# Moving the output product behind the probability transposes, and the value product ahead of the next scores, in a two-pass transformer kernel

## The reference

```python
def _layer(x, wqkv, qs, ksc, wo, lg, lb, w1, b1, w2, b2):
    h = shift_token(x)                      # second half of the columns comes from the row above
    q, k, v = split(h @ wqkv, 3)            # 8 heads of 64
    q, k = l2norm(q) * qs, l2norm(k) * ksc
    q, k = rotary_xpos(q, k)
    o = local_attention(q, k, v)            # windows of 128 rows, own window and the one before
    x = x + o @ wo
    h = layernorm(shift_token(x)) * lg + lb
    a, g = split(h @ w1 + b1, 2)
    return x + (a * gelu(g)) @ w2 + b2
```

## Time and profile before

| | before |
|---|---|
| median of 3 runs | 2546.14 us (2543.6 to 2547.74) |
| the profiled execution | 2547.59 us, of which the span of its instructions is 2545.8 us |
| granted TensorE clock, mean | 0.999 |
| busy: TensorE, VectorE, ScalarE, GpSimd | 98%, 77%, 71%, 61% |

### The profile page before, as it was taken

How to read it: one execution, slowest core, us unless ns; L and a number is a source line. 1 busy time by engine, 2 the same in 40 slices (tenths; PEclk the granted TensorE clock), 3 DMA queues, 4 the chain that set the end, 5 groups by cost and what they waited for, 6 DMA issues and landing times. The chain is left out here.

```text
span 2545.8 us, 80138 instructions
## 1 busy us (share of the span) xinstructions
PE 2489.4 (98%) x29664; PEld 2227.2 (87%) x29664; DVE 1969.8 (77%) x6501; ACT 1816.6 (71%) x5192; POOL 1565.2 (61%) x1799
## 2 busy tenths in 40 slices
PE   8999999999999999999999999999999999999999
PEld 7789888888899889998777888999999988999998
DVE  7888788777777887777655887777777788778886
ACT  5778777777777777776454778777777777777775
POOL 5666666666666666665212667666666667666665
PEclk9999999999999999999999999999999999999999
DMA  3121011003000000005101000000003100000000
GB/s 125 35 85 66 26 57 55 27 21 122 15 2 2 2 2 27 3 9 202 36 19 35 2 2 2 2 2 2 2 2 114 43 3 19 19 19 19 19 19 27
DMA packets 75958, 82.21 MB, mean 32 GB/s; under 512 B 37553, under 2 KB 61873, under 8 KB 74417
## 3 DMA queue, kind: packets, MB, share of 16 engines
q1 hardware_dynamic: 74272, 75.61, 9.1%
...
## 5 line engine op out<-in xcount | busy, mean ns | idle before, releaser
L634 POOL TENSOR_TENSOR pr<-pr,rden 128x384 f32<-128x384 f32 (+1 forms) x480 | 409.4, 870 | 316.3 <-DVE rden L1766 314.3
L842 ACT ACTIVATE pr<-pr,nb 128x192 f32<-128x192 f32 (+1 forms) x1024 | 438.0, 430 | 158.9 <-DVE nb L1757 158.9
L1147 PE MATMUL bank<-h2T,w 128*128 128x256 f32 x1408 | 405.3, 288 | 4.0
L1148 PE MATMUL bank<-h2T,w 128*128 128x256 f32 x1408 | 395.1, 281 | 0.0
L1149 PE MATMUL bank<-h2T,w 128*128 128x256 f32 x1408 | 395.1, 281 | 0.0
L1757 DVE CUSTOM_DVE_ANT_0 pr<-bank,maskb,r 128x192 f32<-128x192 f32 (+1 forms) x1024 | 348.0, 396 | 19.6 <-PE bank L1210 7.9
L676 POOL TENSOR_TENSOR uTl<-t,uTh 128x256 fp32r<-128x256 f32 x288 | 219.5, 767 | 190.7 <-ACT uTh L942 157.6
L1147 PE MATMUL bank<-wqkv,hT 128*128 128x512 f32 x768 | 304.4, 396 | 1.9 <-DVE nb L1757 1.9
L1148 PE MATMUL bank<-wqkv,hT 128*128 128x512 f32 x768 | 302.6, 394 | 0.0
L1149 PE MATMUL bank<-wqkv,hT 128*128 128x512 f32 x768 | 299.8, 390 | 0.0
L1147 PEld LDWEIGHTS bank<-h2T,w 128*128 128x128 f32 x1408 | 266.6, 189 | 11.9 <-DVE h2T L1799 10.5
...
## 6 DMA issues: line engine op xcount, KB each, us to landing
...
stt<-stt SPq DMA_DIRECT2D x256, 3.0 KB
...
stt<-stt SPq DMA_DIRECT2D x192, 0.0 KB
```

The lines of the kernel that those rows point to most:

```text
L634: e.tensor_tensor(probs(j, t), probs(j, t), rden[:, 2 * j:2 * j + 2].unsqueeze(2).to_broadcast([P, 2, w]), ALU.mult).then_inc(pn_done, 1 i ...
L842: last = e.activation(probs(j, t)[:, g, :], probs(j, t)[:, g, :], ACT.Exp, bias=nb[:, hd:hd + 1], scale=-1.0, accum_out=den[:, hd:hd + 1])
L1147: e.matmul(out, left[0], right[0], start=first, stop=False)
L1148: e.matmul(out, left[0], right[1], start=False, stop=False)
```

## The change

It reorders the queues of four engines; no instruction that computes is added or removed, and the sums are the same.

- TensorE: WO of the tile before, which stood between S and A1, goes behind PTE (t = 3) or behind A0 (t = 1, 2). In t = 1 and 2, PV goes behind A2 and the rest of W2, so that the next tile's S follows it. In t = 3 q is transposed ahead of k. In t = 0 two units of W2 go between the transposes of k and of q. W1's job 6 makes the products with the high part of h2T first.
- ScalarE: the square of k goes between the second and the third pair of exponentials (in all tiles; it was so in t = 0 only), without its wait for VectorE's rotary terms. O of the tile before stands behind the exponentials in t = 2 and 3, O_first at the end.
- VectorE: O of the tile before is behind k's chain (t = 2, 3), O_add behind the second reciprocal; k's squares are summed ahead of the third rotary step; the addition of WO and the statistics go behind q's chain.
- GpSimd: the guard of k's norm (`guard_k`) is ahead of the last NP; XB goes behind k's chain in t = 0.
- The small orders: entry normalization and the b1 corrections move by a step or two.

TensorE's queue in an ordinary sequence, from the transposes of t = 2 to its end: before. `h2T`, `hT`, `oT` name the input of W1, A1, WO; `t` is k or q, `pr` the probabilities, `ident` marks a transpose.

The diff, cut to its core:

```diff
@@ -604,6 +604,11 @@
...
         def _(e):
+def guard_k(L, b, t):
+    m = idx(L, b, t)
+    e.wait_ge(ssk_done, at(ssk_done, m + 1))
+    e.tensor_scalar(ssg[:, 0, :], ssk[:, :], 1e-24, None, ALU.max).then_inc(guarded, 1)
 def A1_k(L, b, t):
@@ -611,9 +616,6 @@
...
-    e.wait_ge(ssk_done, at(ssk_done, m + 1))
-    e.tensor_scalar(ssg[:, 0, :], ssk[:, :], 1e-24, None, ALU.max).then_inc(guarded, 1)
     e.wait_ge(guarded, at(guarded, 2 * m + 1))
@@ -683,16 +685,20 @@
...
     for j in range(4 if t else 3):
-        if prev and t == 0 and j == 2:
-            XB(*prev, t)
+        if t == 0 and j == 2:
+            guard_k(*ahead)
         NP(L, b, t, j)
+        if ahead and t and j == 2:
+            guard_k(*ahead)
     if ahead:
         A1_k(*ahead)
+    if prev and t == 0:
+        XB(*prev, t)
     if t == 3:
...
         A1_q(*ahead)
-    if L == 0 and b < 2 and t == 1 - b:
+    if L == 0 and b < B - 1 and t == (1 if b < 2 else 0):
         entry_rstd(b + 1)
@@ -801,11 +806,9 @@
...
-def A1_k(L, b, t, turned=False):
+def A1_k(L, b, t):
     m = idx(L, b, t)
     e.wait_ge(k_ps, at(k_ps, m + 1))
-    if turned:
-        e.wait_ge(rotk, at(rotk, m + 1))
     e.wait_ge(ssk_done, at(ssk_done, m))
@@ -951,33 +954,37 @@
...
         S(L, b, t, j)
-        if t == 0 and j == 1:
+        if ahead and j == 1:
             A1_k(*ahead)
-    if ahead and t:
-        A1_k(*ahead, True)
+    if t > 1:
+        O(L, b, t - 1)
     if ahead:
         A1_qv(*ahead)
-    if L == 0 and b == 0 and t == 2:
-        entry_apply(1, 0)
+    if L == 0 and b < 2 and t == 2:
+        entry_apply(b + 1, 0)
     for a in pair:
...
         A0(*ahead2)
-    if t:
+    if t == 3:
         O_first(L, b, t)
-    if t == 3:
         O(L, b, t)
-    if ahead:
+    if ahead and t == 3:
+        A2_q(*ahead)
+        A2_k(*ahead)
+    elif ahead:
         A2_k(*ahead)
         A2_q(*ahead)
-    if t < 3:
+    if t == 0:
         O(L, b, t)
+    elif t < 3:
+        O_first(L, b, t)
     if t == 3:
...
     if L == 0 and b < B - 1:
-        for k in ((), (0, 1), (2, 3), ())[t] if b else ((), (), (1,), (2, 3))[t]:
+        for k in ((), (0, 1), (2, 3), ())[t] if b > 1 else ((), (), (1,), (2, 3))[t]:
             entry_apply(b + 1, k)
@@ -1220,8 +1227,10 @@
...
         e.wait_ge(pt_sb, at(pt_sb, 3 * n - 2 + a))
-    if j == 0:
+    if j == 0 and t < 2:
         e.wait_ge(o_lo, at(o_lo, 2 * n))
+    elif j == 0:
+        e.wait_ge(o_added, at(o_added, sums(L, b, t - 1) + 2))
     if j == 0 and t == 0:
@@ -1326,7 +1337,17 @@
...
         e.wait_ge(u_done, at(u_done, 12 * b + (96 * L + job - 3)))
-    for g in range(2 if mt < MT - 1 else 1):
+    if job == 6:
+        out = bank[job % 4][:, 0:256]
+        for k in range(KT):
+            for s_ in range(HL):
+                e.matmul(out, w1[:, k, s_, mt * P:(mt + 1) * P], shifted(h2T, 0, k, half * 2 * P, 2 * P),
+                         start=(k == 0 and s_ == 0), stop=False)
+        e.wait_ge(h2t_lo, at(h2t_lo, 2 * b + (16 * L + 2)))
+        for k in range(KT):
+            mm = e.matmul(out, w1[:, k, 0, mt * P:(mt + 1) * P], shifted(h2T, 1, k, half * 2 * P, 2 * P),
+                          start=False, stop=(k == KT - 1))
+    for g in range(0 if job == 6 else 2 if mt < MT - 1 else 1):
         for k in range(KT):
@@ -1389,7 +1410,7 @@
...
         ahead2 = (L, b, t + 2) if t < NT - 2 else nxt and (*nxt, t - 2)
-        cuts = ((5, 6, 11, UNITS), (0, 0, 7, UNITS), (0, 0, 7, UNITS), (0, 0, 7, UNITS))[t]
+        cuts = ((5, 6, 11, 13, UNITS), (0, 0, 7, UNITS), (0, 0, 7, UNITS), (0, 0, 7, UNITS))[t]
@@ -1399,8 +1420,6 @@
...
     S(L, b, t, 1, bool(nxt))
-    if t:
-        WO(L, b, t - 1)
     fill(0)
@@ -1415,17 +1434,29 @@
...
         PTE(L, b, t)
+    if t == 3:
+        WO(L, b, t - 1)
     fill(1)
...
         A0(*ahead2)
-    if t:
+    if t == 0:
+        PV_first(L, b, t)
+        A2(*ahead, 0)
+        fill(2)
+        A2(*ahead, 1)
+        fill(3)
+    elif t < 3:
+        WO(L, b, t - 1)
+        A2(*ahead, 0)
+        A2(*ahead, 1)
+        fill(2)
         PV(L, b, t)
     else:
-        PV_first(L, b, t)
-    if ahead:
-        A2(*ahead, 0)
-        A2(*ahead, 1)
-    fill(2)
+        PV(L, b, t)
+        if ahead:
+            A2(*ahead, 1)
+            A2(*ahead, 0)
+        fill(2)
     if t == 3:
@@ -1954,7 +1985,7 @@
...
         W2(*prev, t - 1)
-    if t:
+    if t == 1:
         O(L, b, t - 1)
@@ -1963,53 +1994,57 @@
...
         R(L, b, t, 1)
+        if L == 0 and b == 0:
+            entry_apply(0, 2)
         squares(idx(*ahead), 0)
...
         rotary(*ahead, 0, (1,))
-        if L == 0 and b == 0:
-            entry_apply(0, 2)
         rotated(*ahead, 0)
...
         squares(idx(*ahead), 1)
-        if L == 0 and b == 1:
-            for j in range(1, 4):
-                entry_stats(b + 1, j)
         A0(*ahead2)
-        if L == 0 and b == 0:
-            entry_stats(1, 1)
+        if L == 0 and b < 2:
+            entry_stats(b + 1, 1)
     else:
-        for j in range(1, 4):
-            if L == 0 and b == 0 and t == 1 and j == 2:
-                entry_apply(0, 3)
-            R(L, b, t, j)
-            if ahead and j == 2:
-                rotary(*ahead, 0)
+        R(L, b, t, 1)
+        if t > 1:
+            for i in pair:
+                O_add(L, b, t - 1, i)
+        if L == 0 and b == 0 and t == 1:
+            entry_apply(0, 3)
+        R(L, b, t, 2)
         if ahead:
+            squares(idx(*ahead), 0)
+            rotary(*ahead, 0, (0,))
+        R(L, b, t, 3)
+        if ahead:
+            rotary(*ahead, 0, (1,))
             rotated(*ahead, 0)
-            squares(idx(*ahead), 0)
-        WO(L, b, t - 1)
+        if t > 1:
+            O(L, b, t - 1)
         if t == 3:
             LN_moments(L, b, 0)
-            halves(L, b, t - 1)
         if ahead:
...
             rotated(*ahead, 1)
+        WO(L, b, t - 1)
+        halves(L, b, t - 1)
         if L == 0 and b == 0 and t == 3:
             beta()
-        if t < 3:
-            halves(L, b, t - 1)
         if ahead2:
             A0(*ahead2)
-        for i in pair:
-            O_add(L, b, t, i)
+        if t == 3:
+            for i in pair:
+                O_add(L, b, t, i)
+    if L == 0 and b < 2 and t == 1:
+        entry_stats(b + 1, 2)
+        entry_stats(b + 1, 3)
     if L == 0 and b == 0 and t == 1:
-        entry_stats(1, 2)
-        entry_stats(1, 3)
         split_lo(4)
```

15 lines of the change are left out of this document (10 added, 5 removed).

## The result

| | before | after |
|---|---|---|
| median | 2546.14 us (2543.6 to 2547.74) | 2681.12 us (2679.06 to 2682.05) |
| ratio, 95% interval | | 1.0532 [1.0518, 1.0545] |
| span of the profiled execution | 2545.8 us | 2677.3 us |
| granted TensorE clock, mean | 0.999 | 0.999 |
| S to S of t = 0, 1, 2, 3 (median of 31 or 32 sequences, from the starts of S) | 10.84, 13.56, 13.45, 33.28 | 11.27, 14.65, 14.44, 35.33 |

The change makes the kernel 5.3% slower. The last row says where: 0.43, 1.09, 0.99 and 2.05 us in the four kinds of tile, 4.56 a sequence. The means over all sequences are a little lower, 0.37, 1.00, 0.89 and 1.99, together 4.24; 32 times that is 136, close to the 131.5 by which the span grew (the last tile of each pass has no A1, and the step from one pass to the other is not in the means). So the loss lies in these tiles.

What follows compares the result with a forecast made beforehand. TensorE's own queue (busy 2489.4 of 2545.8 us) was taken as the bound. Terms 1.0 + 1.0 + 2.4 - 0.33 - 0.1 = 4.0 a sequence, times 32 is 127, less 2, gave 2670 us; range about 2600 to 2705.

Steps and rivals of the forecast that it cites:

- PT waits because WO was its cover: t = 1, 2, 3: without WO's 1.52 us between S and PT, PT's seventh transpose waits for the fourth NP.
- The size of that wait: TensorE reaches PT's seventh transpose 6.43 us after S and waits until 7.3: 0.9 us, in three tiles of four.
- an A1 later than 1.7: Named sign of being wrong: A1 starting later than 1.7 us after S; the forecast start was 1.69.
- R3 behind k's squares and one product costs 0.4: VectorE's third reciprocal starts 6.25 us after S where 5.85 was possible, because of this queue order.
- NP3 at 0.80: GpSimd's fourth normalization takes 0.80 us, not 1.26, ending 7.3 after S; VectorE's addition waits instead.
- slower chain: Rival, chance 0.10: NP3 costs 1.26 or VectorE's first S stays at 1.12; +0.2 to +0.46 in t = 1, 2; about 2700.
- t = 1 and 2 at 14.5: S to S in t = 1 and 2 becomes 14.5 against 13.46 us, +1.0 each, including a small wait for q.
- t = 3, +2.4, less 0.33 in W1: PV of t = 3 starts at 12.1, not 9.69, 1.45 of it a second wait, for WO's addition; W1 saves 0.33.
- one wait only: Rival, chance 0.20: in t = 3 VectorE reaches WO's addition ahead of PV; t = 3 is +0.95, total 2624 us.
- W1's job 6, -0.33: Four high-part products of 0.12 us cover the wait for h2T's low part: -0.33 us a sequence.
- t = 0, -0.1: First tile: XB behind A1_k and the earlier guard free k's chain by 0.2 us, S waits for q's copy; net -0.1.
- The small orders at nothing: Entry normalizations, order of beta and Y additions outside t = 3: no cost, moving within engines 61% to 77% busy.

Runs made afterwards that it cites:

- e4: Kernel before with only TensorE's WO moved behind PTE in t = 1, 2, 3, other engines' orders kept: 2685.06 us, ratio 1.0547.
- e6: Changed kernel with XB back, WO's addition early in t = 3, Square of k later, W2 units between S and A1, ten behind PTE (t = 1, 2): 2565.31 us.
- e2: Changed kernel with VectorE's addition of WO put between q's two rotary products in t = 3 only: 2656.32 us, ratio 1.0435.
- e7: Kernel before with only W1's job 6 changed, high-part products first and the low-part wait behind them: 2541.04 us, ratio 0.9987.
- e1: Changed kernel with GpSimd's XB put back ahead of k's guard in t = 0: 2667.16 us, ratio 1.0477.
- e10: e6 with the third tile's statistics right behind VectorE's addition of WO in t = 3: 2557.36 us, ratio 1.0046.
- e11b: e6 with t = 0 as before, t = 3 reordered (WO between A1 and PT), third tile's statistics behind the first layer norm moments: 2549.39 us, ratio 1.0017.

## Why the prediction came out right

The forecast was 2670 against 2681.12, inside its range, with the case that had most of the chance. The mechanism was right, and the experiments show it; that the sum came so close is in part luck, since terms of both signs were off. By its own steps:

- **PT waits because WO was its cover.** Right. e4 shows it by the move of WO alone, e6 by giving the cover back: t = 1 and 2 go from 14.65 and 14.44 to 13.36 and 13.29.
- **The size of that wait.** NP3 was to end at 7.3 and ended at 7.43; the seventh PT was forecast for 7.3 and came at 7.48. The parts are off in two terms. VectorE's first scores come at 1.00, not 0.9: without the oT rows in its way it waits for the first bank of S all the same. And A1 starts at 1.91, not at 1.69, since bank 0 is given back only after VectorE's second row (745.15 to 745.58) is read. So of the 0.9 that was put ahead of PT, 0.36 stands ahead of A1 (33.5 / 93, the second largest wait) and 0.53 ahead of PT (50.2 / 95), by the brackets. By starts the two cost more than the 0.98 forecast (0.08 and 0.9): 1.15 in t = 2. The prediction had named an A1 later than 1.7 as a sign that it was wrong. It came, at 1.91, and what it refutes is the placing of the wait, not its cause: e4 and e6 show the cover.
- **R3 behind k's squares and one product costs 0.4.** It came 6.36 after S, against 6.25, and 0.43 behind the read-out of the last Exp (5.93).
- **NP3 at 0.80.** It measured 0.83, with VectorE's addition behind it at 0.84 instead of 0.69. Of the "slower chain" rival the half with NP3 at 1.26 is out; the other half came in part, with VectorE's first scores at 1.00, between 0.9 and 1.12. The Trainium skill, page "SBUF — State Buffer", in the part on the two physically separate sides, has GpSimd and VectorE take the shared port pair for whole instructions, the first to start winning, where a VectorE instruction with two SBUF inputs meets a GpSimd one that reads SBUF. By that rule, the trace agrees on who wins, in t = 0 too, where XB came first and the addition took 1.12. It does not agree to the end. The one behind was 0.11 to 0.15 us shorter than strictly one after the other would make it: NP3 in the earlier trace rows 1.26 and not 0.80 + 0.57, the addition 0.84 and not 0.98, behind XB 1.12 and not 1.27. And a power that GpSimd had started first held no addition up, as the last section shows.
- **t = 1 and 2 at 14.5.** 14.65 and 14.44, by terms that were off and cancel. In t = 2 the lost cover cost 1.15 and not 0.98, the new place of PV gave 0.33 and not 0.2, and the further wait of 0.3 for q measured 0.11 in A2 and 0.06 in WO. Less than that 0.33 is left as a gain of the tile in e6 (0.20 and 0.17), since small waits remain there.
- **t = 3, +2.4, less 0.33 in W1.** PV was to start 12.1 after S; it started 12.08 after (758.54 to 770.62). The split was wrong again: 0.94 of waiting ahead of PV (30.1 us in 30 places), not 1.45, since TensorE itself got there at about 11.1 and not at 10.65, through A1 and PT. e2 confirms the second wait: -0.97 in t = 3. The "one wait only" rival is out.
- **W1's job 6, -0.33.** e7: 33.28 to 32.95.
- **t = 0, -0.1.** Wrong: +0.43. The step that failed is "XB behind A1_k ... free the k chain". It looked at what XB left and not at where it went: XB now meets the addition of q, which A2 and S wait for. e1 shows 0.30 of it. By the means it is 0.47 a sequence, 15 us; t = 2 and t = 3 gave 0.11 and 0.08 less than forecast and take 6 of it back. The span ended 6.5 above the forecast, and the rest of the 11 us lies between the span and the median.
- **The small orders at nothing.** In the changed kernel they could not be seen behind the large waits. In e10 and e11b one of them, the late statistics, is worth 0.26 to 0.77 in t = 3. The statistics were not even on the list, and "they move within engines that are 61% to 77% busy" is no price: they have DMAs and a layer norm behind them.

What stays open: what each of the three things that e6 changed together in t = 1 and 2 gives by itself, what holds WO back behind PTE in t = 3, and why runs of e7 have more stretches at the low clock.
